# Second layer of a four-layer graph network: three products with the edge frame summed by TensorE in the transpose instead of by VectorE

## The reference, cut to what matters

```python
R = jax.nn.relu(abs_distances[:, None] @ w1 + b1) @ w2 + b2
Y = spherical_harmonics(rel_vec)
Fj = features[src]
...
acc = acc + _NORM[i] * jnp.einsum('euv,ef,evi,ofi->euo', Rb[..., k], Yf, Fb, C)
...
out = out.at[dst].add(msg)
```

## Time and profile before

| | |
|---|---|
| runs without profile, median (range) | 21037.66 us (21004.45 to 21056.62) |
| profiled execution | 20949.39 us |
| its span, first to last instruction | 20947.3 us |
| second layer in it (first to last radial product) | 6691.1 to 12434.6 us |
| busy over the span: TensorE, VectorE, POOL | 62%, 53%, 56% |
| mean granted TensorE clock | 0.733 of full speed |

### The profile page before, as it was taken

The page is one execution under the profiler, slowest core; times in us unless marked ns, Lnnn a source line. Parts: engine busy times, 40 slices in busy tenths (PEclk is TensorE's granted clock), DMA queues, the critical chain, the costliest instruction groups (busy, mean ns, idle before and its releaser), DMA issues. The chain is left out here.

```text
span 20947.3 us, 295438 instructions
## 1 busy us (share of the span) xinstructions
PE 13050.8 (62%) x92471; PEld 7352.1 (35%) x92471; DVE 11193.0 (53%) x19689; ACT 3069.2 (15%) x5120; POOL 11774.1 (56%) x10055
## 2 busy tenths in 40 slices
PE   0565555555554676777676653555555555699999
PEld 0344334333333444444444431222212112355554
DVE  2565544444443777777777773223233222567777
ACT  0222222222221111111111110111111111000000
POOL 4788888888886555555555555666666665100000
PEclk6555555555556888888888876666666666899999
DMA  7344444444444222222221112333333333478887
GB/s 277 48 39 37 37 38 38 37 38 36 37 38 45 48 49 47 49 48 48 48 48 46 47 40 36 71 72 72 73 70 72 70 74 68 129 258 292 290 292 267
DMA packets 3778481, 1817.19 MB, mean 87 GB/s; under 512 B 2956642, under 2 KB 3551915, under 8 KB 3758859
## 3 DMA queue, kind: packets, MB, share of 16 engines
q1 hardware_dynamic: 1777244, 1336.91, 22.7%
q0 software_dynamic: 669312, 166.80, 9.9%
q10 hardware_dynamic: 1330864, 300.38, 7.8%
HBM read 1474.43 MB, written 392.90 MB: 89 GB/s over the span
## 5 line engine op out<-in xcount | busy, mean ns | idle before, releaser
L1996 POOL DMA_INDIRECT xg<-d_tab,s_i x3136 | 3245.5, 1035 | 2560.6 <-POOLq L1987 1561.8
L2536 POOL DMA_INDIRECT xg<-d_tab,s_i x3136 | 3002.1, 957 | 1890.8 <-issue 957.7
L2256 PE MATMUL pR<-w,H 128*128 128x384 f32 x6272 | 2679.3, 556 | 1375.3 <-PEq L2250 831.2
L1394 POOL DMA_INDIRECT d_acc<-AG,ix x1568 | 2465.6, 1572 | 527.2 <-issue 467.8
L1394 POOL DMA_INDIRECT d_acc<-T,ix x1568 | 2465.1, 1572 | 523.1 <-issue 442.3
L2924 PE MATMUL pacc<-nodes,HB 128*32 128x512 fp8e4 x47040 | 2662.3, 380 | 54.6 <-PEq L2968 54.6
L2573 DVE TENSOR_TENSOR_SCAN U<-mU,U,up 128x512 f32<-128x512 f32 x392 | 501.6, 1280 | 3316.9 <-DVEq L2572 2829.8
L2256 PEld LDWEIGHTS pR<-w,H 128*128 128x128 f32 x6272 | 1213.8, 213 | 2476.0 <-issue 2122.7
L2696 PE MATMUL hb<-U,Wbc 128*128 128x512 f32 x784 | 653.7, 930 | 2194.1 <-PEq L2690 1985.1
L1747 PE MATMUL pm<-ms,eq 128*128 128x32 f32 x6272 | 1363.9, 399 | 922.6 <-PEq L1745 922.3
L2924 PEld LDWEIGHTS pacc<-nodes,HB 128*32 128x32 f16 x47040 | 1263.2, 97 | 1326.9 <-issue 68.8
(11 more groups left out here) (338 smaller groups left out, 17488.3 us busy)
## 6 DMA issues: line engine op xcount, KB each, us to landing
packed<-d_A SPq DMA_DIRECT2D x420, 1792.0 KB
row<-d_m SPq DMA_DIRECT2D x1568, 64.0 KB
xg<-d_tab,s_i POOLq DMA_INDIRECT x6272
wrow<-d_w SPq DMA_DIRECT2D x196, 512.0 KB
d_scan<-so ACTq DMA_DIRECT2D x392, 256.0 KB
d_A<-stage ACTq DMA_DIRECT2D x97, 784.0 KB, 10.9
d_ea<-in_ea_t ACTq DMA_DIRECT2D x1, 50176.0 KB
d_exp<-T ACTq DMA_DIRECT2D x1, 50176.0 KB, 246.6
```

The lines of the kernel that those rows point to most:

```text
L1394: e.indirect_dma_start(out=d_acc[i], out_offset=bass.IndirectOffsetOnAxis(ap=ix[k][:, t:t + 1], axis=0), in_=mo[k][:, t * F:(t + 1) * F], ...
L1996: e.indirect_dma_start(out=xg[k][:, t, :], out_offset=None, in_=d_tab, in_offset=bass.IndirectOffsetOnAxis(ap=s_i[n][:, t:t + 1], axis=0)) ...
L2256: last = e.matmul(pR[u % 2][:, j, 0:384], H[k][:, (2 * u + j) * P:(2 * u + j + 1) * P], w2[:, :], start=True, stop=True)
L2536: e.indirect_dma_start(out=xg[n][:, j * ST + c, :], out_offset=None, in_=d_tab, in_offset=bass.IndirectOffsetOnAxis(ap=s_i[d][:, col:col + ...
```

## The change

- `tail` becomes one part, behind product 1. It issues three products of 384 elements, one for each axis, that go straight into three images of the message tile, `mg[k][:, i, :, 8:32]`; `tv`, both additions and their two waits go.
- `mg` grows from one to three images for each of its two buffers. The scalars stay in image 0; the scalar places of images 1 and 2 are set to zero once, ahead of the loop.
- `columns` issues, instead of four transposes, twelve plain products with the identity, three for each of the four columns, which add up in `tp`.

```diff
@@ tiles @@
-            mg = [sb(st, f"mg{k}", [P, T, F]) for k in range(2)]
-            tv = sb(st, "tv", [P, 3, T, 8, 3])
+            mg = [sb(edges, f"mg{k}", [P, 3, T, F]) for k in range(2)]
@@ vector, ahead of the loop @@
+                    for k in range(2):
+                        e.memset(mg[k][:, 1:3, :, 0:8], 0.0).then_inc(S("vc"), 1)
...
@@ vector, tail @@
-                            e.tensor_tensor(tv[:, :, :, :, :], bc(Q[k][:, 1:4, :, :], 4, 3), bc(e9[n][:, :, :, :], 3, 8),
-                                            ALU.mult).then_inc(S("tz"), 1)
-                        elif part == 1:
-                            e.wait_ge(S("tz"), 1)
...
-                            e.tensor_tensor(by_stream(mg[k])[:, :, :, 8:32], of[:, 0, :, :, :], of[:, 2, :, :, :], ALU.add
-                                            ).then_inc(S(f"mg{k}"), 1)
+                        for i in range(3):
+                            to = mg[k][:, i, :, 8:32].rearrange("p (j c) (u o) -> p c j u o", c=ST, o=3)
+                            axis = e9[n][:, i, :, :].rearrange("p (c j) o -> p c j o", c=ST)
+                            last = e.tensor_tensor(to, bc(Q[k][:, 1 + i, :, :].rearrange("p (c j) u -> p c j u", c=ST), 4, 3),
+                                                   bc(axis, 3, 8), ALU.mult)
+                        last.then_inc(S(f"mg{k}"), 1)
@@ vector, step @@
-                                if u in (1, 2, 3):
-                                    tail((n + 3) % 4, u - 1)
+                                if u == 1:
+                                    tail((n + 3) % 4)
@@ tensor, columns @@
-                            last = e.transpose(tp[k][:, j * P:(j + 1) * P],
-                                               mg[k][:, j * ST:(j + 1) * ST, :].rearrange("p c f -> p (c f)"), ident[:, :])
+                            for i in range(3):
+                                last = e.matmul(tp[k][:, j * P:(j + 1) * P],
+                                                mg[k][:, i, j * ST:(j + 1) * ST, :].rearrange("p c f -> p (c f)"), ident[:, :],
+                                                start=(i == 0), stop=(i == 2))
```

More of the change, by code:

```diff
@@ L2020, in _ @@
                         e.sem_inc(S("vc"), -1)
+                    for k in range(2):
+                        e.memset(mg[k][:, 1:3, :, 0:8], 0.0).then_inc(S("vc"), 1)
+                        e.wait_ge(S("vc"), 1)
+                        e.sem_inc(S("vc"), -1)
                     e.memset(w2[64:P, :], 0.0).then_inc(S("vc"), 1)
@@ L2082, in sums, with tail @@
                                         ).then_inc(S("vq"), 1)
-                    def tail(n, part):
+                    def tail(n):
                         k = n % 2
[L2086 to L2091, removed]
-                            e.tensor_tensor(tv[:, :, :, :, :], bc(Q[k][:, 1:4, :, :], 4, 3), bc(e9[n][:, :, :, :], 3, 8),
-                                            ALU.mult).then_inc(S("tz"), 1)
-                        elif part == 1:
-                            e.wait_ge(S("tz"), 1)
[L2096 to L2102, removed]
-                            e.tensor_tensor(by_stream(mg[k])[:, :, :, 8:32], of[:, 0, :, :, :], of[:, 2, :, :, :], ALU.add
-                                            ).then_inc(S(f"mg{k}"), 1)
+                        e.wait_ge(S("vq"), 3)
+                        e.sem_inc(S("vq"), -3)
+                        e.wait_ge(S(f"fmg{k}"), 1)
+                        e.sem_inc(S(f"fmg{k}"), -1)
+                        e.sem_inc(S("qd"), 1)
+                        for i in range(3):
[4 more added lines that the diff above has]
+                        last.then_inc(S(f"mg{k}"), 1)
                     def scan(n):
@@ L2145, in _ @@
                     e.sem_inc(S("qc"), -1)
-                    for part in range(3):
-                        tail(3, part)
+                    tail(3)
                     scan(3)
@@ L2199, in scalars @@
                         e.sem_inc(S("qd"), -1)
-                        e.activation(by_stream(mg[k])[:, :, :, 0:8], Q[k][:, 0, :, :].rearrange("p (c j) u -> p c j u", c=ST),
+                        e.activation(by_stream(mg[k][:, 0, :, :])[:, :, :, 0:8], Q[k][:, 0, :, :].rearrange("p (c j) u -> p c j u", c=ST),
                                      ACT.Copy).then_inc(S("ms"), 1)
```

## The result

The changed kernel takes 21885.6 us (21877.98 to 21887.57, four runs) against 21047.14 us for the kernel before on the same chip. The ratio is 1.0385, with a 95% interval of 1.0365 to 1.0405: 838 us slower, where 488 us were forecast, and inside the range.

What follows compares the result with a forecast made beforehand. VectorE was taken to bound full groups, TensorE close behind, and TensorE to set standing groups' pace at product 5; 0.37 x 1.62 + 0.63 x 3.0 = 2.49 us, times 196, added 488 to 21037.66: about 21,525 us, range 21,000 to 22,000.

Steps and rivals of the forecast that it cites:

- `columns` stands between radial 4 and radial 5: TensorE's added records delay radial 5, which product 5 awaits: 1.62 us more in a full group.
- The count: In `columns`, twelve plain products make 24 TensorE records, 20 more than the four transposes.
- the cost of VectorE's products: In VectorE's tail, three products of 0.47 us each, 1.40 us instead of 2.20, saving 0.80 us in a group.
- The pace of 0.11 us: In `columns`, time between TensorE records at full clock; 20 more cost 2.24 us, or 4.48 at half clock.
- the relief buys nothing: The 0.80 us saved on VectorE ahead of product 4 only bring it earlier to the wait for radial 5.
- the two kinds of group: Second layer: full groups, VectorE always busy, 21.53 us, share 0.37; standing groups, with long waits, 34.02 us, 3.0 us added.
- the last rival: Full groups turn into standing ones as POOL catches up; half turning adds 453 us, about 21,980 us; chance 0.10.
- What moves: Around `columns`: earlier `mg` raises the frame's release a little earlier, load order stays, no wait is added; no cost priced.
- the rival in which the relief helps POOL: Less VectorE work delays POOL's gathers less, ending the standing 0.80 us sooner in a group: 20,880 us; chance 0.13.

Runs made afterwards that it cites:

- The pair without the standing: Kernels before and after the change, each with eight gathers in a group instead of sixteen: 19536.44 and 19855.71 us.
- the pair with a late `half`: Kernels before and after the change, with the signal starting POOL's second eight gathers raised at radial product 5 instead of 3: 20589.67 and 20927.66 us.
- a_eight: The kernel after with eight gathers in a group instead of sixteen: 19855.71 us, ratio 0.9508.
- a_four: The kernel after with four transposes of the first image only, so VectorE's part of the change alone: ratio 1.0139.
- a_fe_late: The kernel after with the edge frame's release raised behind radial product 5 instead of ahead of the twelve products: ratio 1.0348.
- b_half5: The kernel before with the signal that lets POOL begin its second eight gathers raised at radial product 5 instead of 3: 20589.67 us, ratio 0.9859.

## Why the prediction was right, and where it was off

*Right: what is on the path.* The step "`columns` stands between radial 4 and radial 5" priced a full group at 1.62 us more. The pair without the standing gives 319 us, 1.63 us in each of 196 groups, and the pair with a late `half` 338 us. The count (24 records for 4) and the cost of VectorE's products (busy time down by 157 us) came out as written. The pace of 0.11 us came out without the standing, 0.112 in `a_eight`; in the kernel after half of the records follow at 0.21 us or more.

*Wrong: the relief buys nothing.* The fit of 1.63 to 1.62 is partly luck. In the groups of equal length TensorE's part costs 1.8 us and the relief gives back 0.6, so that the whole costs 1.16 us there; the wait ahead of product 0, once in a turn, brings the mean to 1.68. The prediction held radial 5 fixed while VectorE got earlier. But by the code the radial products wait for banks that VectorE frees, so that a faster VectorE can move TensorE too.

*Wrong, and hidden by luck: the two kinds of group.* The sum kept the share of full groups at 0.37, with 1.62 us more in each, and gave the standing ones 3.0 us each: 117 and 370 us in all. The traces, group by group from one product 0 to the next, show otherwise (28 us lies in the gap between the two kinds; in the kernel before only two groups are between 26 and 30 us):

| | groups over 28 us | their mean | other groups | their mean |
|---|---|---|---|---|
| before | 119 of 195 | 33.46 us | 76 | 22.94 us |
| after | 191 of 195 | 33.97 us | 4 | 26.08 us |

Counted from scan to scan it is 118 and 189 long groups of 194, with means of 34.00 and 33.92 us. The share was read rightly (76 of 195 are 0.39), but it did not stay. 72 more groups stand, at 33.97 - 22.94 = 11.0 us each, or 794 us; a standing group is longer by only 0.5 us on the mean, 61 us for 119 of them. Together that is nearly all of the 4.44 us in a group. So the loss is the last rival's, full groups that turn into standing ones, not for half of them but for nearly all. It had a chance of 0.10. The forecast of 488 us came near 838 because a term far too large stood in for one that was missing. The step that failed is the sum's share of 0.37, taken as it was before the change, together with "What moves", which set an earlier `mg` and a shorter tail at nothing; `a_four`, which has just these, costs 1.4%.

The gathers go with it, as that rival's reason has it. Count as one run what POOL issues without a pause of over 2.5 us. Before, there are 97 runs of 16 gathers, 40 of 32 and 5 of 48: POOL is often so far behind that it goes straight on into the next group. After, 189 of 194 runs are of 16, so POOL stops in nearly every group; with eight gathers nearly all runs are of four. VectorE waits for more than 4 us ahead of a product 126 times before and 198 times after, and 92% and 94% of these waits end only after the start of a run's last gather. Which of the two drives the other these counts do not say.

*Fell: the rival in which the relief helps POOL.* Gathers did get faster, 989 ns on the mean instead of 1035, in line with the page "SBUF — State Buffer" of the Trainium skill, section "SBUF: two separate sides". But the mean does not show the cause: `a_fe_late`, with the same relief, has 1038 ns, and `b_half5`, without it, 1017. POOL turned what it gained into waiting: 2509 us for a free buffer in place of 1486 in the same stretch (L1986 after, L1987 before). That a POOL further ahead is what makes more groups stand fits `a_four` (gathers at 1009 ns) and the late `half`, but no run changed the gathers' pace alone, so it is argued, not shown. Shown is that the standing goes with half the gathers, and moves with their start.

## What to carry to other kernels

Work taken off the busiest engine is worth what the next wait on its path leaves of it; price the work that goes to the other engine by the place where it stands in that engine's order, here two records per plain f32 product against one per transpose, right ahead of an awaited result. Where a stage has idle time that several engines share, find out first what starts and ends it: here the phase of a fourth engine's gathers was worth 3.7% in the kernel after (ratios 1.0385 and 1.0017), nearly as much as the whole change cost, and one index moved it. Where a stage has two kinds of group, ask first whether a change moves groups from one kind to the other, and only then what it adds to each. And take a change apart: the half that looked harmless cost 1.4%.

## Unexpected in the hardware

While POOL issues a long run of gathers, TensorE, VectorE, ScalarE and SyncE can all slow down at once, for about ten microseconds in the group shown, and recover some three after the start of the last gather: of VectorE's 198 waits of over 4 us in the kernel after, half end 3.6 us or more behind the start of the gather before. VectorE then stays at a wait whose result was ready long before (radial 4 ended at 9108.44, product 4 began at 9120.20), and four small loads take SyncE 7.76 us to issue. Of these waits 137 begin behind the start of the tenth or eleventh gather of a run; but a run can also pass there without one, as in the full group of the earlier trace rows. With 16 gathers in a group the kernel before takes 29.39 us for it, with eight 22.15. It is not that the DMA engines are full: they are busy for 0.14 of the stretch from 9110 to 9120, at 31 GB/s. What the engines share in that time no run here shows.
